# Rotary attention in a two-layer kernel: the scores as three fp32r products of split keys and queries, with spreads moved to the score banks and query projections to another place

## The reference, cut to what matters

```python
q, k, v = layer_norm(x), layer_norm(ctx), layer_norm(ctx)      # ctx: 2 x 128 rows
qh, kh, vh = (heads(q @ Wq), heads(k @ Wk), heads(v @ Wv))     # 16 heads of 64
qh, kh = rope(qh), rope(kh)
aw = einsum('nhtd,nhTd->nhtT', qh, kh) / sqrt(64)
aw = 30 * tanh(aw / 30)
aw = where(pad | causal, -inf, aw)                             # t < 128 only is cut by causal
out = einsum('nhtT,nhTd->nhtd', softmax(aw), vh)
x = x + merge(out) @ Wo
```

## Time and profile before

| | us |
|---|---|
| median of three runs | 1525.1 |
| lowest, highest | 1524.49, 1525.53 |
| the profiled execution | 1526.41 |
| its span in the profile | 1524.6 |
| TensorE busy | 1454.5 |
| VectorE busy | 1205.0 |
| ScalarE busy | 878.9 |
| GpSimd busy | 504.8 |

### The profile page before, as it was taken

How to read it: one execution, slowest core, us unless ns; L and a number is a source line. 1 busy time by engine, 2 the same in 40 slices (tenths; PEclk the granted TensorE clock), 3 DMA queues, 4 the chain that set the end, 5 groups by cost and what they waited for, 6 DMA issues and landing times. The chain is left out here.

```text
span 1524.6 us, 30064 instructions
## 1 busy us (share of the span) xinstructions
PE 1454.5 (95%) x10610; PEld 1074.7 (70%) x10634; DVE 1205.0 (79%) x2421; ACT 878.9 (58%) x2090; POOL 504.8 (33%) x442
## 2 busy tenths in 40 slices
PE   7899999999999999799998998999999989998996
PEld 5677777777777777544443467788888877776885
DVE  5688888897888765688878968888888886786875
ACT  2444444444444443656567837788888886774442
POOL 0122222222222221200003745454545545665333
PEclk9999999999999999999999999999999999999998
DMA  8511111110111101123305710000000024325641
GB/s 288 185 46 45 45 45 45 45 41 8 36 42 35 45 8 77 46 95 133 152 1 208 309 40 3 3 1 3 3 4 3 4 66 176 122 106 181 200 152 59
DMA packets 47807, 118.34 MB, mean 78 GB/s; under 512 B 9422, under 2 KB 15950, under 8 KB 46032
## 3 DMA queue, kind: packets, MB, share of 16 engines
q1 hardware_dynamic: 42016, 100.03, 18.6%
q0 software_dynamic: 5680, 16.85, 2.8%
HBM read 78.90 MB, written 39.80 MB: 78 GB/s over the span
## 5 line engine op out<-in xcount | busy, mean ns | idle before, releaser
L1819 ACT ACTIVATE c_probs<-c_score,c_minus_top 128x128 f32<-128x128 f32 x512 | 183.2, 420 | 4.7 <-DVE c_minus_top L1955 4.5
L1769 POOL TENSOR_TENSOR c_probs<-c_probs,c_recip 128x1024 f32<-128x1024 f32 x64 | 121.6, 1900 | 164.9 <-DVE c_recip L1961 164.9
L699 POOL TENSOR_TENSOR a_attn_lo_parts<-a_attn,a_attn_hi_parts 128x512 fp32r<-128x512 f32 x64 | 80.5, 1295 | 251.5 <-ACT a_attn_hi_parts L761 251.5
L1819 ACT ACTIVATION_READ_ACCUMULATOR c_probs<-c_score,c_minus_top 128x1 f32 x512 | 133.3, 260 | 0.0
L757 ACT COPY a_attn<-a_pv_ps 128x512 f32<-128x512 f32 x64 | 36.9, 577 | 165.7 <-PE a_pv_ps L1059 165.7
L1446 POOL TENSOR_TENSOR xres<-xres,b_delta 128x512 f32<-128x512 f32 x24 | 48.3, 2025 | 209.3 <-DVE b_delta L1503 209.3
L430 PE MATMUL a_bank<-a_x_hi_parts,a_wq_hi 128*128 128x256 f32 x512 | 107.4, 291 | 0.3 <-PEq L445 0.3
L430 PE MATMUL a_bank<-a_x_lo_parts,a_wq_hi 128*128 128x256 f32 x512 | 103.4, 283 | 0.0
L430 PE MATMUL a_bank<-a_x_hi_parts,a_wq_lo 128*128 128x256 f32 x512 | 102.9, 283 | 0.0
L1027 PE MATMUL a_bank<-a_wo_hi,a_attn_hi_parts 128*128 128x512 f32 x256 | 102.7, 401 | 0.0
L1029 PE MATMUL a_bank<-a_wo_hi,a_attn_lo_parts 128*128 128x512 f32 x256 | 101.2, 395 | 0.0
(11 more groups left out here) (352 smaller groups left out, 4329.3 us busy)
## 6 DMA issues: line engine op xcount, KB each, us to landing
hidden<-b_hidden SPq DMA_DIRECT2D x5, 2816.0 KB, 8.1
b_hidden<-hidden SPq DMA_DIRECT2D x5, 2816.0 KB, 10.7
xres<-in_x SPq DMA_DIRECT2D x8, 1024.0 KB, 14.3
d_we<-in_we SPq DMA_DIRECT2D x8, 1024.0 KB, 7.4
xres<-in_w_gate_up SPq DMA_DIRECT2D x7, 1024.0 KB, 5.4
d_got<-rows SPq DMA_DIRECT2D x20, 258.0 KB, 2.9
xres<-rows SPq DMA_DIRECT2D x19, 258.0 KB, 3.0
a_rot<-in_rot SPq DMA_DIRECT2D x16, 256.0 KB, 3.1
```

The lines of the kernel that those rows point to most:

```text
L699: nc.gpsimd.tensor_tensor(of_spread(attn_lo, g), of_spread(attn, g), of_spread(attn_hi, g), ALU.subtract).then_inc(attn_lo_ready, 1)
L1769: nc.gpsimd.tensor_tensor(part, part, recip[:, t % 2, heads].unsqueeze(2).to_broadcast([P, HALF, KEYS]), ALU.mult).then_inc(scaled, 1)
L1819: last = nc.scalar.activation(probs[:, t, at, :], score_ps[:, h, g, :], ACT.Exp, bias=minus_top[:, h, g:g + 1], accum_out=total[:, t, at:a ...
```

## The change

- **Scores.** The keys are kept as a high part in fp32r (`keys_hi`) and the rest (`keys_lo`), made in the preparation by ScalarE and GpSimd. For each unit ScalarE copies the rotated queries to `q_hi` (`query_high`) and GpSimd makes `q_lo` (`query_low`) in place of `q`. `scores` sums high by high, low keys by high queries, and high keys by low queries: 12 products in fp32r on the same half-row tiles, in the same banks.
- **Spreads** go to the score banks (`spread_bank`), all but the last chunk's, once ScalarE has capped what was there; so the first scores of the next chunk wait until VectorE has weighed with them.
- **Projections** 2 and 3 of the next chunk are done at the end of a chunk, 2 ahead of its first two scores and 3 behind them; before the first chunk likewise.
- **Room.** Raw keys, and keys and values of the first batch entry, lie in rows of `xres` that later hold x; so four pieces of x are loaded in the preparation, the last of them behind a wait for the low keys, and two in the ninth chunk.
- **Order elsewhere.** ScalarE takes the exponentials of the next chunk's unit 0 behind the high parts of the attention, and raw values 3 before them. VectorE weighs all four at once, masks unit 0 of the first chunk later, and rotates groups 2 and 3 behind a wait for the scores that read the buffer. At the stage's end three of six weight groups are turned ahead of the first spread (`weights_ahead`), and the first output takes all high parts before the low parts (`output_high_first`).

```diff
+        def in_rows(name, tile, tiles, dt):
+            return nc.alloc_sbuf_tensor_at("a_" + name, [P, tiles, ROW], dt, offset=xres_offset + 4 * ROW * tile)[:, :, 0:D]
+
+        keys_raw = in_rows("keys_raw", TILE_KEYS, B * ROW_KEYS, F32)
+        keys_hi = [in_rows("keys_hi0", TILE_HI, ROW_KEYS, F32R), sb("keys_hi1", [P, ROW_KEYS, D], F32R)[:]]
+        keys_lo = [in_rows("keys_lo0", TILE_LO, ROW_KEYS, F32R), sb("keys_lo1", [P, ROW_KEYS, D], F32R)[:]]
+        vals = [in_rows("vals0", TILE_VALS, 2, F32), sb("vals1", [P, 2, D])[:]]
+        q_hi = sb("q_hi", [P, 2, 2, ROPE_CHUNK], F32R)
...
+        def spread_bank(n, g):
+            if isinstance(n, int) and n == NC - 1:
+                return ring.use(n, 0, plan(n)[f"B{g}"]).out[:]
+            return score_ps[:, g // 2, 2 * (g % 2):2 * (g % 2) + 2, :]
...
+                        if c == TILE_KEYS // TPC:
+                            sp.wait_ge(q_lo_ready, BLOCKS)
                         load_x(c, ld_x)
 
...
+                    for pair in range(BLOCKS // 2):
+                        for b in range(B):
+                            pool.wait_ge(q_hi_ready, 2 * pair + b + 1)
+                            nc.gpsimd.tensor_tensor(key_pair(keys_lo[b], pair), raw_pair(b, pair), key_pair(keys_hi[b], pair), ALU.subtract).then_inc(q_lo_ready, 1)
...
+                    for pair in range(BLOCKS // 2):
+                        act.wait_ge(q_ready, 2 * pair + 2)
+                        for b in range(B):
+                            nc.scalar.copy(key_pair(keys_hi[b], pair), raw_pair(b, pair)).then_inc(q_hi_ready, 1)
...
+                    if n == CPBA:
+                        sp.wait_ge(pv_full, UNITS * CPBA)
+                        for c in range(TILE_HI // TPC, CHUNKS - 1):
+                            sp.dma_start(xres[:, c * TPC:(c + 1) * TPC, 0:D],
+                                         io["x"][c * CHUNK:(c + 1) * CHUNK, :].rearrange("(t p) f -> p t f", p=P)).then_inc(ld_x, 16)
...
+                def query_low(n, g):
+                    pool.wait_ge(q_hi_ready, BLOCKS + n * UNITS + g + 1)
+                    nc.gpsimd.tensor_tensor(q_lo[:, g % 2], q[:, g % 2], q_hi[:, g % 2], ALU.subtract).then_inc(q_lo_ready, 1)
...
+                        query_low(n, 2)
+                        query_low(n, 3)
+                    if "X0" in s:
                         for k in range(2):
                             x_low(n + 1, k)
+                        query_low(n + 1, 0)
+                        query_low(n + 1, 1)
                     if "B0" in s:
                         for g in range(4):
                             attn_low(n, g)
...
+                def query_high(n, g):
+                    act.wait_ge(q_ready, BLOCKS + n * UNITS + g + 1)
+                    nc.scalar.copy(q_hi[:, g % 2], q[:, g % 2]).then_inc(q_hi_ready, 1)
...
-                    if not (isinstance(n, int) and n == 0 and g == 0):
-                        dve.wait_ge(q_ready, n * UNITS + g)
+                    dve.wait_ge(q_ready, BLOCKS + n * UNITS + g)
+                    if g >= 2:
+                        dve.wait_ge(score_full, n * UNITS + g - 1)
                     nc.vector.tensor_tensor(q[:, g % 2], src[:], by_angle(0), ALU.mult)
...
                         for g in range(2):
                             rotate_begin(*queries(g, n + 1))
-                            rotate_end(n + 1, g, use(f"Q{g}").emptied[1])
-                    if "Q2" in s:
-                        weigh(0)
-                        weigh(1)
+                            rotate_end(n + 1, g, query_taken(g))
+                    if "B0" in s:
+                        for g in range(4):
+                            weigh(g)
+                    if "O0" in s:
+                        row_stats(1)
                     if "X0" in s:
                         mask(n + 1, 0)
-                    if "Q2" in s:
-                        weigh(2)
-                        weigh(3)
-                    if "O0" in s:
...
+                def scores(n, b, p, spread_taken=None):
                     unit = n * UNITS + p
-                    pe.wait_ge(q_ready, unit + 1)
-                    if p >= 2 or not isinstance(n, int) or n >= 1:
+                    pe.wait_ge(q_hi_ready, BLOCKS + unit + 1)
+                    if p >= 2:
                         pe.wait_ge(capped, unit - 1)
-                    for h in range(4):
-                        rows, m = slice(h % 2 * DH0, (h % 2 + 1) * DH0), 2 * p + h // 2
-                        last = nc.tensor.matmul(score_ps[:, p % 2, place(h), :], keysT[rows, m, b * KEYS:(b + 1) * KEYS], q[rows, p % 2, h // 2, :],
-                                                start=True, stop=True)
+                    elif spread_taken is not None:
+                        pe.wait_ge(freed["dve"], spread_taken)
+                    if isinstance(n, int) and n == 0 and p == 0:
+                        pe.wait_ge(q_lo_ready, BLOCKS)
+                    for part, (keys, queries) in enumerate(((keys_hi[b], q_hi), (keys_lo[b], q_hi), (keys_hi[b], q_lo))):
+                        if part == 2:
+                            pe.wait_ge(q_lo_ready, BLOCKS + unit + 1)
+                        for h in range(4):
+                            rows, m = slice(h % 2 * DH0, (h % 2 + 1) * DH0), 2 * p + h // 2
+                            last = nc.tensor.matmul(score_ps[:, p % 2, place(h), :], keys[rows, m // 4, m % 4 * KEYS:(m % 4 + 1) * KEYS],
+                                                    queries[rows, p % 2, h // 2, :], start=(part == 0 and h < 2), stop=(part == 2 and h >= 2))
                     last.then_inc(score_full, 1)
...
-                first_turn = ring.use(0, 0, plan(0)["Q2"])
+                project(begin_first(PRE_Q + 2), 2)
                 scores(0, 0, 0)
-                pe.wait_ge(freed[first_turn.reuse[0]], first_turn.reuse[1])
-                project(first_turn.out, 2)
+                project(begin_first(PRE_Q + 3), 3)
                 scores(0, 0, 1)
...
-                        out = [begin(f"B{2 * m + i}") for i in range(2)]
+                        if isinstance(n, int) and n == NC - 1:
+                            out = [begin(f"B{2 * m + i}") for i in range(2)]
+                        else:
+                            pe.wait_ge(capped, n * UNITS + 3 + m)
+                            out = [spread_bank(n, 2 * m + i) for i in range(2)]
                         for i in range(2):
...
+                    def output_high_first():
+                        out, tokens = begin("O0")[:].rearrange("p a c -> p (a c)"), slice(0, P)
+                        for k in range(BLOCKS):
+                            if k % (BLOCKS // 2) == 0:
+                                pe.wait_ge(attn_hi_ready, UNITS * (n - 1) + (2 if k == 0 else UNITS))
+                            high = attn_hi[:, k // 4, k // 2 % 2, k % 2, tokens]
+                            nc.tensor.matmul(out, high, wo_hi[:, k, :], start=(k == 0), stop=False)
+                            nc.tensor.matmul(out, high, wo_lo[:, k, :], start=False, stop=False)
+                        for k in range(BLOCKS):
+                            if k % (BLOCKS // 2) == 0:
+                                pe.wait_ge(attn_lo_ready, UNITS * (n - 1) + (2 if k == 0 else UNITS))
+                            last = nc.tensor.matmul(out, attn_lo[:, k // 4, k // 2 % 2, k % 2, tokens], wo_hi[:, k, :], start=False, stop=(k == BLOCKS - 1))
+                        last.then_inc(bank_full, 1)
+
+                    def weights_ahead(groups):
+                        pe.wait_ge(ahead.loaded, 16)
+                        pe.wait_ge(ahead.ident_ready, 1)
+                        pe.wait_ge(capped, UNITS * NC)
+                        for g in groups:
+                            ahead.turn(nc, g, turn_places[g])
...
-                        pe.wait_ge(ahead.loaded, 16)
-                        pe.wait_ge(ahead.ident_ready, 1)
-                        pe.wait_ge(capped, UNITS * NC)
                         pe.wait_ge(raw_ready, UNITS * NC)
-                        for g in range(ahead.GROUPS_AHEAD):
-                            ahead.turn(nc, g, turn_places[g])
-                    if "O0" in s:
+                        weights_ahead(range(GROUPS_EARLY, ahead.GROUPS_AHEAD))
+                        output_high_first()
+                    elif "O0" in s:
...
-                    if "Q2" in s:
+                        spread(0)
                         values(n, b, 2)
-                    if "X0" in s:
-                        scores(n + 1, b_next, 0)
-                    if "Q2" in s:
+                        spread(1)
+                        values(n, b, 3)
+                        project(begin_queries(2), 2)
+                        for p in range(2):
+                            scores(n + 1, b_next, p, ring.use(n, 0, s[f"B{2 * p + 1}"]).emptied[1])
+                        project(begin_queries(3), 3)
+                        values(n + 1, b_next, 0)
```

(7 more changed lines are left out.)

128 lines of the change are left out of this document (77 added, 51 removed).

## The result

| | before | changed |
|---|---|---|
| median | 1524.58 us (5 runs) | 1531.89 us (5 runs) |
| the profiled execution | 1526.41 us | 1529.45 us |
| ratio, 95% interval | | 1.0057 [1.0045, 1.0068] |

Slower by some 7 us, where 1515.4 was forecast. The two profiled executions differ by 3.0 us only: the one of the changed kernel was its fastest, and behind the rotary stage, where both run the same code, it was 2.9 us quicker. So I compare within the stage. Its end is the first use of the row scale on TensorE. The stage accounts for 5.9 us of the 7; the rest lies between executions and isn't placed.

The account below looks back on a forecast made before the run. It took TensorE's stream to bound the rotary stage, with other engines handing over in time. Scores -10.5, first chunk +3.0 and stage's end -2.2 sum to -9.7 us: 1525.1 to 1515.4 us, range 1508 to 1530.

Parts of the forecast that it names:

- Scores, -10.5: Rotary stage on TensorE: a group of scores in fp32r takes 0.88 us instead of 1.06, over 60 groups: -10.5 us.
- The weight-load rule: Score products: a load overlaps running matmuls only when going to another row group, so a group would be longer than before.
- Rivals 1 and 3: Scores: fp32r halves or loads don't overlap, 1557 us, chance 0.08; rounds take about 0.147, 1525.9 us, chance 0.12.
- So the move of projections costs nothing on TensorE by itself.: Middle chunk: moving projections leaves 18 changes of the array's tiling before and after, so it costs 0.
- The handover margins: Middle chunk: first scores have 1.4 us to spare, second scores 0.9, their low queries 1.4, so new work hides.
- Rival 2: Handover becomes the bound: second first-scores wait for weighing 3; 1.2 us of wait a chunk gives 1533 us; chance 0.10.
- Preparation. Cover: about 2 us: Before the main part: added copies and GpSimd subtractions fit ahead of TensorE's need for x_lo, about 2 us spare, no cost.
- First chunk, +3.0: First chunk: last sums start at 72.9 us instead of 69.91, +3.0 us; TensorE idles some 5.5 us.
- Stage's end, -2.2: Rotary stage's end: three of six weight groups turned in TensorE's wait for the reciprocals, path 1.1 instead of 3.4: -2.2 us.

Follow-up runs that it names:

- the f32 run: Changed kernel with four f32 products of the high parts in place of twelve, low parts left out of the scores: 1541.0 us, ratio 1.0124.
- The split output: Kernel with low keys on VectorE and values 2 ahead of the spreads, plus sums of unit 0 moved to the middle of output 0: 1521.75 us.
- the second experiment: Changed kernel with the values of unit 2 ahead of the first spread on TensorE instead of behind it: 1525.69 us, ratio 1.0017.
- the fill: Changed kernel with VectorE filling the low query weights with zeros instead of subtracting: 1523.59 us, ratio 0.9999.
- the kernel with both edits: Changed kernel with the low-key subtractions moved from GpSimd to VectorE and values 2 ahead of the spreads: 1519.82 us, ratio 0.9977.

## Why the prediction was wrong

- **Scores, -10.5.** The form was right, and the f32 run shows that it counts to the end. A group fell from 1.06 or 1.07 to 0.91 us, which is 0.62 a chunk and 9.2 us over 15 chunks. The forecast had 0.88: a round was right to 0.001 us, but what a group takes beyond its rounds is 0.20 and not 0.18. The weight-load rule weighed there (the Trainium skill, TensorE: Matmul & The Clock Gate, Part 3, The mechanism) doesn't hold in this trace if it is taken alone: the second product of each half goes to the same rows, and the rounds still follow every 0.118 us. The same section also lets a load run ahead into a background weight buffer, and with that the trace agrees. Rivals 1 and 3 are out. The prediction speaks of two rounds of an f32 group and prices four, one for each pair of records; the price is borne out, since a second f32 group beside the first adds 1.93 - 1.07 = 0.86 us.
- **"So the move of projections costs nothing on TensorE by itself."** This step failed, by a small amount. The count of 18 changes of tiling before and after is right, but it takes each for worth the same. Of stretches of whole-array work there are seven instead of six: two are split off and one is joined to a spread, and by the steps above that costs 0.32 us a chunk. The two score groups side by side give 0.20 back, as the prediction said. What is left is 0.12 a chunk, 1.8 us over 15. The split output confirms the price of a border, 0.19 us for leaving and entering, on outputs.
- **The handover margins.** Those I worked out held: no wait ahead of the scores in a middle chunk. The wait that came was for one that I had not listed, and this step cost the chunks most. I followed scores, weighings and low queries, not the raw copy between values 2 and values 3, which lost its cover when the scores of the next chunk moved from between them. Its 0.30 to 0.38 us add up to 5.3 us over 15 chunks, and the second experiment took them back. Rival 2 had the right kind (a small wait, paid 15 times) with the wrong place and size.
- **The change of the batch entry.** 1.3 us more where the forecast had a gain, for which no run was made. The mask's row explains 0.4 of it, by a wait of values 0; the cause of the rest is open. Against the pattern of the other chunks it is 1.4 us long. So -9.2, +1.8, +5.3 and +1.4 make -0.7 of the -1.0 us measured, where -10.5 was forecast; the other 0.3 lie in the first of these intervals and aren't placed.
- **"Preparation. Cover: about 2 us" and a cost of nothing.** This step failed worst in a single place, by 7.3 us, and without it the stage would be 1.4 us faster than before instead of 5.9 slower. The GpSimd time was sized well (8 x 0.75 us forecast; 5.91 in all beside the fill) and the gap of 6.1 us was there, but I looked only at GpSimd's row for a free stretch. VectorE's 4.42 us subtraction lies in the same stretch, and the two don't run together. A missing cover was to move the start by what is missing; it was 5.6 us of wait, and the slow clock behind it added 1.7.
- **First chunk, +3.0.** It measured +2.1. The idle time was 4.8 us, not 5.5. Right in kind.
- **Stage's end, -2.2.** It measured -2.46, of which the three groups are 1.65.

The range reached to 1530, and the measured time is 1.9 us beyond it. It left out most of rival 2 (1533 at 1.2 us of wait a chunk), and that rival's figure lies near the measured time by luck only, since the wait was 0.4 us and most of the rest is the preparation's. The preparation had no spread of its own, though GpSimd's free stretch of 6.1 us was to be filled with 6.0 us of work.

## What to carry to other kernels

A free stretch on GpSimd is cover for a subtraction only if VectorE isn't running one that reads two SBUF tiles there; look at both rows before moving a subtraction. When work is moved out from between two steps on a tuned TensorE stream, list every pair that it stood between and ask what the second one waits for, copies out of PSUM among it. And on an in-order engine put the copy whose input is ready ahead of the one that waits: that was worth 6 us here against the same kernel without it, and, with values 2 moved ahead of the projections, it took the kernel with both edits from 1519.8 to 1516.1 us.

## What the runs showed of the hardware

- VectorE and GpSimd can shut each other out, by what the two instructions read. A GpSimd subtraction of 128x256 took 4.91 us instead of 0.73 beside VectorE's subtraction of two SBUF tiles, and 0.74 (at most 0.92) while VectorE's fill ran. It goes the other way too: the mask took 1.82 us instead of 0.69, and the slower of the two row products of the next x (a `tensor_scalar` from SBUF) up to 1.04 us instead of 0.54. VectorE's rotations, which read one operand from PSUM, kept their 0.69 and 0.68 us beside GpSimd. The Trainium skill states this (SBUF — State Buffer, Who interferes with whom): the shared port pair is an exclusive lock, taken for a whole instruction by whoever issues first. A VectorE instruction with two SBUF inputs wants it against a GpSimd instruction that reads SBUF, and so can a `tensor_scalar`, in a mode that uses two ports. The trace agrees in each of these rows. The prediction had not weighed it for a preparation in which both engines subtract.
- Entering whole-array work from narrower tiles cost projections and outputs about 0.1 us, and leaving it as much (output 5.60, 5.71 and 5.80 us with none, one and both). It isn't the same for all work: a turn of x takes 0.53 us behind an output and 0.59 alone, and a spread takes 0.54 behind a projection as well as alone.
- fp32r products on half the rows run in pairs, 0.118 us a pair of 256 columns (597.73 - 596.11 less 573.83 - 572.91, for six pairs).
- An idle time of 5.7 us before the main part was followed by the lower clock (0.50) for 4.4 us; one of 1.6 us at the same place, in the kernel with the low keys on VectorE, was not (1.00).
